# Shared-expert gate and up products of a transformer block: float32 operands replaced by two scaled float16 parts

## The chip, the cores and the metric

The kernel is one program on one core of a Trainium2 chip. The core has a matrix engine (TensorE, PE in the rows, with its weight loads as PEld), a vector engine (VectorE, DVE), an activation engine (ScalarE, ACT), a general engine (GpSimd, POOL), a sequencer that issues most of the DMAs here (SyncE, SP), and 16 DMA engines. Each engine runs its own list of instructions in order; semaphores tie the lists together. The metric is device time in microseconds (us), less is better, as the median of several runs.

## What is computed

The block takes x of 2 x 2048 tokens with 256 channels and gives x of the same shape. Cut to what matters:

```
x = x + ga * attention(layernorm(x) * (1 + ca) + sa)       # 16 heads of 16, q/k/v/o with LoRA parts
h = layernorm(x) * (1 + cb) + sb                           # sa ... gb: modulation, per batch
shared = (silu(h @ shared_gate.T) * (h @ shared_up.T)) @ shared_down.T      # 512 hidden
logits = h @ gate_w.T ; e = argmax(logits) ; s = sigmoid(max(logits))       # 8 experts, one per token
routed = swiglu_e(h * s)                                   # expert e's own gate, up and down weights
x = x + gb * (shared + routed)
```

The change concerns `h @ shared_gate.T` and `h @ shared_up.T`: 4096 tokens x 256 channels x 512 outputs, twice.

## The kernel before, in words

The program has five stages, each written as one function per engine (`attend_tensor`, `attend_vector` and so on).

**Setup and projection** (until about 130 us): adapters are folded into the weights, q, k and v are made.

**Attention** (`attend_*`) runs over 32 heads (16 heads x 2 batches), 37 us a head. For each head TensorE makes the products whose row maxima VectorE finds (`max_product` L1237, `reduce_pair` L1374, 32 pairs m of two blocks a head), up to two heads ahead of the head that is being weighed. Three PSUM banks form a ring between the two: TensorE may not write the next block before VectorE (or, for one block in eight, ScalarE, L1416) has released a bank. Between these blocks TensorE issues, in an order written by hand in `turn`, the scores (L1293) that ScalarE exponentiates (L1437) and the weighing of v by them (L1305). GpSimd has small tasks once a head (`attend_gpsimd`) and a few large ones in named heads: it adds a bias to rows of x (L1490) and divides heads by their sums (L1532). SP loads what later stages need in the function `prepare(n)`.

**Merge** (`merge_*`, from about 1305 us) runs over 8 groups g of 512 tokens: output projection (L1652), residual (DVE L1721), layernorm statistics, normalized rows `n2` (ACT L1764), transposition of them (PE L1661), modulation into `h2T` (ACT L1772, `take`), router logits. Its last part holds the gate and up products of group 0 and the routing on VectorE (`route_vector`). SP stores `x1` and `n2` to DRAM here, loads `wgT`, and then the expert weights: `rgT`, `ruT` and `rdT`, 17 transfers of 512 KB (L1598 to L1602).

**Shared expert** (`shared_*`, 1362 to 1514 us). A group needs four units of gate and up (`gate_up`, L1622: in a unit 2 weights x 2 halves of the 256 channels, 512 columns each), ScalarE's silu (L1981), VectorE's product `hid` (L1825), and `down` (L1959). TensorE's order is gate_up(g+1), down(g), gate_up(g+2), down(g+1) and so on, and it may be at most two units ahead of VectorE: a unit waits until `s_gu_free` shows that the unit two before it has been multiplied. VectorE's order is residual(g) (L1996, then L2000, which needs the loaded rows `xr` of group g), and only then `hid` for group g+2. After the last group's units and down(6) comes the transposition of the first routed tile (L2065, it needs that tile's rows `xs`), then down(7), then the routed experts.

Beside this, GpSimd scatters the 32 tiles of normalized rows into expert order (`scatter_gpsimd`, L1929 to L1942), four buffers `sc_x` deep. SP feeds both: its list (`shared_sync`) is `token_rows` (four loads of `sc_x`, L1894, each of which waits until the scatter from that buffer has landed) in turn with `store(g)` (L1898) and `load(g+2)` (the rows `xr`, L1888). So the order is token_rows(0), load(0), load(1), token_rows(1), then for g in 0 to 2: token_rows(2g+2), store(g), load(g+2), token_rows(2g+3); then store(3), load(5), the wait for all scatters, four loads of `xs` (L2050), store(4), load(6), store(5), load(7), store(6), store(7).

**Routed experts** (`routed_*`, to the end): 39 tiles of 128 rows, each with its expert's weights (L2086, L2109).

## Time and profile before

| | us |
|---|---|
| median of the runs before (1747.12 to 1748.29) | 1747.13 |
| the profiled execution, device time | 1743.12 |
| its span in the trace | 1741.1 |
| TensorE busy | 1681.1 (97%) |
| VectorE busy | 1374.7 (79%) |
| ScalarE busy | 1332.6 (77%) |
| GpSimd busy | 333.1 (19%) |

Times in the trace run from the start of the span. A row of the order of time gives the start, the length, the engine, the line, the operation, its tiles and, in square brackets, how long the engine sat idle before it and what ended the idling. SPq is SP's DMA queue; a row of it is the issue, not the transfer. A matmul's end is modelled, so its pace is read from one start to the next.

### The profile page before, as it was taken

How to read it: one execution, taken by the hardware profiler on the slowest of the kernel's cores; microseconds unless marked ns; L12 is line 12 of the kernel's file. 1: busy time of each engine (PE TensorE's matmuls, PEld its weight loads, DVE VectorE, ACT ScalarE, POOL GpSimd, SP SyncE). 2: the span in 40 equal slices, each digit the busy share in tenths (PEclk: the TensorE clock that was granted, in tenths of full speed). 3: DMA queues.
4: the chain of work that ended last, by engine and by line, in shares of the span. 5: the costliest groups of instructions: out<-in, count | busy, mean ns of one | idle time of the engine just before them, and what ended most of it. 6: DMA issues, size and time to landing. Idle time of an engine off the chain costs nothing.

```text
span 1741.1 us, 31097 instructions
## 1 busy us (share of the span) xinstructions
PE 1681.1 (97%) x11097; PEld 650.6 (37%) x11098; DVE 1374.7 (79%) x2723; ACT 1332.6 (77%) x1662; POOL 333.1 (19%) x427
## 2 busy tenths in 40 slices
PE   9999999999999999999999999999989999999997
PEld 5532222222222222222222222222217555799996
DVE  7689999999999999999999999999906422355553
ACT  5449999999999999999999999999997211244442
POOL 5525020040000000000001000001010377133332
PEclk9999999999999999999999999999999999999998
DMA  7322021131110111101322001131025633322221
GB/s 234 99 66 74 30 80 34 70 93 42 43 58 22 31 52 34 34 22 34 92 61 55 22 31 33 48 88 38 27 78 217 266 107 122 118 74 67 66 69 39
DMA packets 76509, 124.93 MB, mean 72 GB/s; under 512 B 15652, under 2 KB 49141, under 8 KB 76252
## 3 DMA queue, kind: packets, MB, share of 16 engines
q1 hardware_dynamic: 67628, 99.33, 18.3%
q0 software_dynamic: 7792, 22.57, 3.9%
q8 instruction: 77, 1.26, 0.3%
q10 hardware_dynamic: 960, 1.34, 0.3%
q14 instruction: 52, 0.43, 0.1%
HBM read 76.50 MB, written 47.21 MB: 71 GB/s over the span
## 4 chain that ended last, share of the span: by engine, by line
PE 82%; DVE 10%; ACT 5%; issue 3%; DMA 0%; POOLq 0%; POOL 0%; ACTq 0%; DVEq 0%
PE ps L1305 27%; PE ps L1237 18%; DVE mx L1374 8%; PE ps L2086 8%; PE ps L1293 8%; PE ps L1622 6%; PE ps L2109 4%; ACT prob L1437 4%; PE ps L1959 3%; PE ps L780 3%; PE ps L1652 2%; PE ps L799 2%; ACT step_sb L1416 1%; PE ps L2065 0%; PE ps L1266 0%
## 5 line engine op out<-in xcount | busy, mean ns | idle before, releaser
L1437 ACT ACTIVATE prob<-ps 128x1024 f32<-128x1024 f32 x1024 | 1000.8, 1049 | 75.0 <-PE ps L1293 74.8
L1374 DVE TENSOR_REDUCE mx<-ps 128x1 f32<-128x512 f32 x1558 | 1000.7, 685 | 64.0 <-PE ps L1237 43.4
L1237 PE MATMUL ps<-k_high,q_high 48*128 48x512 f16 x1803 | 545.5, 383 | 24.3 <-DVE mx L1374 0.2
L1305 PE MATMUL ps<-prob,vs 128*32 128x512 f32 x4096 | 545.5, 605 | 4.3 <-ACT prob L1437 3.5
L1293 PE MATMUL ps<-q_high,k_high 50*128 50x512 f16 x2048 | 419.0, 382 | 1.6 <-ACT prob L1437 1.6
L1237 PEld LDWEIGHTS ps<-k_high,q_high 48*128 48x128 f16 x1803 | 128.9, 93 | 596.6 <-DVE mx L1374 413.4
L1371 DVE CUSTOM_DVE_ANT_0 step_sb<-ps,step_sb 128x512 f32<-128x512 f32 x245 | 166.8, 681 | 0.0
L1293 PEld LDWEIGHTS ps<-q_high,k_high 50*128 50x128 f16 x2048 | 100.4, 94 | 168.5 <-ACT prob L1437 161.3
L1466 POOL CAST mb<-turned_sb 16x128 f16<-16x128 f32 x32 | 9.0, 280 | 768.6 <-ACT turned_sb L1423 755.1
L1416 ACT ACTIVATE step_sb<-ps 128x512 f32<-128x512 f32 x245 | 150.6, 615 | 0.2 <-PE ps L1237 0.2
L1305 PEld LDWEIGHTS ps<-prob,vs 128*32 128x32 f32 x4096 | 80.6, 107 | 167.5 <-issue 140.1
L1981 ACT ACTIVATE sgate<-ps 128x512 f32<-128x512 f32 x32 | 19.1, 597 | 117.4 <-PE ps L1622 117.4
L2135 ACT ACTIVATE esig<-ps 128x512 f32<-128x512 f32 x39 | 23.3, 597 | 111.4 <-PE ps L2086 111.4
L2169 DVE TENSOR_TENSOR ehT<-esig,ps 128x512 f32<-128x512 f32 x39 | 26.8, 688 | 98.9 <-PE ps L2086 98.9
L1237 PE MATMUL ps<-k_step,q_high 48*128 48x512 f16 x245 | 94.7, 386 | 0.0
L1825 DVE TENSOR_TENSOR hid<-sgate,ps 128x512 f32<-128x512 f32 x32 | 22.0, 688 | 72.5 <-ACT sgate L1981 72.1
L2086 PEld LDWEIGHTS ps<-xsT,gate_w 128*128 128x128 f32 x624 | 75.6, 192 | 1.9
L2086 PE MATMUL ps<-xsT,up_w 128*128 128x128 f32 x624 | 76.0, 275 | 0.0
L2086 PE MATMUL ps<-xsT,gate_w 128*128 128x128 f32 x624 | 76.0, 275 | 0.0
L2109 PE MATMUL ps<-rdT,ehT 128*128 x312 | 73.6, 379 | 0.0
L2086 PEld LDWEIGHTS ps<-xsT,up_w 128*128 128x128 f32 x624 | 72.8, 192 | 0.0
L2229 POOL DMA_INDIRECT x_in<-x_rows,cix x39 | 37.7, 967 | 153.0 <-DVE eout L2196 110.0
(195 smaller groups left out, 1407.7 us busy)
## 6 DMA issues: line engine op xcount, KB each, us to landing
qk_parts<-parts SPq DMA_DIRECT2D x32, 256.0 KB, 2.4
k_high<-qk_parts SPq DMA_DIRECT2D x63, 128.0 KB, 2.7
head_out<-head_out_sb SPq DMA_DIRECT2D x31, 256.0 KB, 2.5
sorted_in<-zero_row POOLq DMA_DIRECT2D x13, 390.0 KB, 3.7
xs<-sorted_in SPq DMA_DIRECT2D x39, 130.0 KB
xg<-in_x SPq DMA_DIRECT2D x8, 512.0 KB, 5.4
x_rows<-xg SPq DMA_DIRECT2D x8, 512.0 KB, 5.0
n_rows<-n SPq DMA_DIRECT2D x8, 512.0 KB, 4.0
```

Source lines behind the costliest of these rows:

```text
L780: mm = pe.matmul(ps[:, 2 + n % 2, :], wqkv[:, o // 2, k, (o % 2) * P:(o % 2 + 1) * P], hT[g % CPB][:, k, :], start=(k == 0), stop=(k == 1))
L1237: pe.matmul(ps[:, ring.bank((n, m, u)), :], q_high[p][mine, t * P:(t + 1) * P], keys, start=True, stop=True).then_inc(s_max, 1)
L1293: mm = pe.matmul(ps[:, bank + u, :], k_high[p][mine, kt * P:(kt + 1) * P], q_high[p][mine, i * CH:(i + 1) * CH], start=True, stop=True)
L1305: mm = pe.matmul(ps[32 * j:32 * j + 32, 7, :], vs[buf(h)][:, kt, :], prob[:, (kt + 1) % 2, j * CH:(j + 1) * CH], start=(kt == 0), stop=(kt ...
L1371: dve.tensor_tensor_reduce(step_sb[:], bank, step_sb[:], 1.0, LOWEST, ALU.add, ALU.max, largest).then_inc(s_ring, 1)
L1374: dve.tensor_reduce(largest, bank, AX.X, ALU.max).then_inc(s_ring, 1)
L1416: act.activation(step_sb[:], bank, ACT.Relu).then_inc(s_turned, 1)
L1437: act.activation(prob[:, (kt + 1) % 2, :].rearrange("p (u c n) -> p u c n", u=2, c=2)[:, :, half, :], ps[:, bank:bank + 2, :], ACT.Exp, sc ...
L1622: mm = pe.matmul(ps[:, at, :], w[:, k, fc * P:(fc + 1) * P], h2T[:, k, bass.ds(g * CH, CH)], start=(k == 0), stop=(k == 1))
L1959: mm = pe.matmul(ps[:, DOWN_BANK[u] + t // 2, t % 2 * D:(t % 2 + 1) * D], hid[u][:, fc, t * P:(t + 1) * P], wdT[:, fc, :], start=(fc == 0) ...
L2086: mm = pe.matmul(ps[:, bank, fc * P:(fc + 1) * P], w[u][:, c, fc * P:(fc + 1) * P], xsT[u][:, c, :], start=(c == 0), stop=(c == 1))
L2109: mm = pe.matmul(ps[:, 6 + u, 0:D], ehT[u][:, c, :], rdT[:, bass.ds(e, 1), c, :].squeeze(1), start=(c == 0), stop=(c == FC - 1))
```

## The change

1. The float32 weights `wgT` and `wuT` are no longer held. They are loaded as `raw_gate` and `raw_up` in head 9 of attention, together with `wdT` (three transfers of 512 KB in place of two), and the load of `wgT` in the merge goes.
2. VectorE finds the largest magnitudes of both weights and of the modulation factors in head 12 (`largest_value`, three reductions). SP stores them in head 13 and loads them back, spread to all partitions, in head 14. In head 17 VectorE makes powers of two from them (`ffn_units`, nine small operations in a row).
3. GpSimd scales `colffn` and splits `raw_gate` in head 18 and `raw_up` in head 19, three passes over 128 x 1024 each (`split_weights`), into `wg_parts` and `wu_parts`, a high and a low float16 part.
4. In the merge `h2T` is two buffers of one group each in place of one tile for all. GpSimd splits each group into `h2_parts` (`split_rows`, two operations over 128 x 1024 a group); ScalarE's `take` waits until the group two before has been split.
5. A gate or up product of a half is three float16 matmuls (high x high, high x low, low x high) in place of one float32 matmul. The scales are taken back in ScalarE's silu (`scale=`), in `take_logits`, and in VectorE's `hid` (a scalar_tensor_tensor in place of a tensor_tensor).
6. The last two of the eight `rdT` loads lie where the `h2T` buffers were. They move from the end of the merge's list on SP to behind token_rows(1) of `shared_sync`, behind waits for the last logits and the last split.

```diff
...
-                    for dst, name in ((wuT, "wuT"), (wdT, "wdT")):
+                    for dst, name in ((raw_gate, "wgT"), (raw_up, "wuT"), (wdT, "wdT")):
...
+                if n == TOPS_AT + 1:
+                    sp.wait_ge(s_range, 10)
+                    sp.dma_start(tops_dram, tops[:]).then_inc(s_shared, 16)
...
+        TOP_TURNS = (8, 14, 20)
...
+            dve.tensor_reduce(tops[:, i:i + 1], source, AX.X, ALU.max, apply_absolute_value=True).then_inc(s_range, 1)
...
+                    if n == TOPS_AT and m in TOP_TURNS:
+                        largest_value(dve, TOP_TURNS.index(m))
+                    if n == TOPS_AT + 5 and m == TOP_TURNS[0]:
+                        ffn_units(dve, step)
...
+            step(pool.tensor_tensor(flat, flat, ffn_scale[:, i:i + 1].to_broadcast([P, HALF * F]), ALU.mult))
+            step(pool.tensor_copy(high, flat))
+            pool.tensor_tensor(low, flat, high, ALU.subtract).then_inc(s_range, 1)
...
-            sp.dma_start(wgT[:], io["wgT"]).then_inc(s_shared, 16)
...
-            for e in range(E):
+            for e in range(E - 2):
                 sp.dma_start(rdT[:, e:e + 1], io["rdT"][:, e:e + 1]).then_inc(s_expert_late, 16)
...
-            for w, at in ((wgT, bank), (wuT, bank + 1)):
+            for w, at in ((wg_parts, bank), (wu_parts, bank + 1)):
...
-                    mm = pe.matmul(ps[:, at, :], w[:, k, fc * P:(fc + 1) * P],
-                                   h2T[:, k, bass.ds(g * CH, CH)], start=(k == 0), stop=(k == 1))
+                    for wp, hp in ((0, 0), (0, 1), (1, 0)):
+                        mm = pe.matmul(ps[:, at, :], w[:, wp, k, fc * P:(fc + 1) * P],
+                                       h2_parts[:, bass.ds(g, 1), hp, k, :].squeeze(1), start=(k == 0 and hp + wp == 0),
+                                       stop=(k == 1 and wp == 1))
...
                 act.wait_ge(s_n2T, g + 1)
+                wait(act, s_h2_parts, g - 1)
+                wait(act, s_lgp, g - 1)
...
             token_rows(1)
+            sp.wait_ge(s_lgp, NCH)
+            sp.wait_ge(s_h2_parts, NCH)
+            for e in range(E - 2, E):
+                sp.dma_start(rdT[:, e:e + 1], io["rdT"][:, e:e + 1]).then_inc(s_expert_late, 16)
             for g in range(3):
...
+        def split_rows(pool, step):
...
+                pool.wait_ge(s_h2T, g + 1)
+                step(pool.tensor_copy(high, flat))
+                pool.tensor_tensor(low, flat, high, ALU.subtract).then_inc(s_h2_parts, 1)
...
```

How the instructions stand, at three places. On VectorE in attention, in head 12 around pairs 8 and 14 (`mx` holds the maxima; the ISA rows at L1371, L1393 in the change, are the one block in eight that is folded with `step_sb`), before:

```order
L1371 ISA step_sb,mx_78<-ps,step_sb 128x512
L1371 ISA mx_78 128x1
L1374 TENSOR_REDUCE mx_78<-ps 128x1 x6
L1371 ISA step_sb,mx_78<-ps,step_sb 128x512
L1371 ISA mx_78 128x1
```

and in the change:

```order
L1396 TENSOR_REDUCE mx_79<-ps 128x1 x5
L1416 TENSOR_REDUCE tops<-raw_gate 128x1
L1396 TENSOR_REDUCE mx_79<-ps 128x1
L1393 ISA step_sb,mx_79<-ps,step_sb 128x512
L1393 ISA mx_79 128x1
L1396 TENSOR_REDUCE mx_79<-ps 128x1 x6
L1393 ISA step_sb,mx_79<-ps,step_sb 128x512
L1393 ISA mx_79 128x1
L1396 TENSOR_REDUCE mx_79<-ps 128x1
L1416 TENSOR_REDUCE tops<-raw_up 128x1
```

Each run of reductions is cut once by a reduction over a weight; in head 17 the nine operations of `ffn_units` stand in such a gap all in a row.

On SP at the start of the shared expert (the two rows in front of `sc_x` are the end of the expert weights), before:

```order
L1600 DMA ruT<-in_ruT 128x1024 x8
L1602 DMA rdT<-in_rdT 128x1024 x8
L1894 DMA sc_x_204<-n_rows 128x256
L1894 DMA sc_x_205<-n_rows 128x256
L1894 DMA sc_x_206<-n_rows 128x256
L1894 DMA sc_x_207<-n_rows 128x256
L1888 DMA xr_200<-x_rows 128x1024
L1888 DMA xr_201<-x_rows 128x1024
```

and in the change, up to where token_rows(2) begins:

```order
L1669 DMA ruT<-in_ruT 128x1024 x8
L1671 DMA rdT<-in_rdT 128x1024 x6
...
L1962 DMA xr_210<-x_rows 128x1024
L1962 DMA xr_211<-x_rows 128x1024
L1968 DMA sc_x_214<-n_rows 128x256
L1968 DMA sc_x_215<-n_rows 128x256
L1968 DMA sc_x_216<-n_rows 128x256
L1968 DMA sc_x_217<-n_rows 128x256
L1982 DMA rdT<-in_rdT 128x1024 x2
```

Two of the eight large loads have moved from in front of the first `sc_x` loads to behind the second four; nothing else on SP's list of this stage has moved, the loads of `xr` least of all.

On TensorE, three units in the middle of a group's loop body, before (each matmul is float32):

```order
L1622 MATMUL ps<-h2T,wgT 128x512 x2
L1622 MATMUL ps<-h2T,wuT 128x512 x2
L1617 REGISTER_ALU
L1622 MATMUL ps<-h2T,wgT 128x512 x2
L1622 MATMUL ps<-h2T,wuT 128x512 x2
L1959 MATMUL ps<-wdT,hid_173 128x256 x16
```

and in the change (float16):

```order
L1692 MATMUL ps<-h_parts,wg_parts 128x512 x6
L1692 MATMUL ps<-h_parts,wu_parts 128x512 x6
L1686 REGISTER_ALU
L1692 MATMUL ps<-h_parts,wg_parts 128x512 x6
L1692 MATMUL ps<-h_parts,wu_parts 128x512 x6
L2046 MATMUL ps<-wdT,hid_183 128x256 x16
```

A unit has 12 float16 matmuls where it had 4 float32 ones; `down` is as it was.

## Rows read from the trace of the kernel before

**Rows 1.** Page, part 4: the chain that ended last, shares of the span by line.

```profile
PE ps L1305 27%; PE ps L1237 18%; DVE mx L1374 8%; PE ps L2086 8%; PE ps L1293 8%; PE ps L1622 6%; PE ps L2109 4%; ACT prob L1437 4%; PE ps L1959 3%; PE ps L780 3%; PE ps L1652 2%; PE ps L799 2%; ACT step_sb L1416 1%; PE ps L2065 0%; PE ps L1266 0%
```

**Rows 2.** Windows of one head each: stretch, length, busy PE, PEld, DVE, ACT, POOL, clock, DMA.

```profile
685.80:722.80 37.00, 35.81 (x261) 7.86 (x257) 35.18 (x66) 34.59 (x44) 1.85 (x5) 1.00 0.12 37
796.70:833.90 37.20, 35.82 (x261) 8.02 (x257) 35.49 (x69) 34.59 (x43) 1.85 (x5) 1.00 0.16 50
```

**Rows 3.** Order of time, VectorE, in the second of these heads.

```profile
822.26 0.34 DVE L1071 RECIPROCAL sums<-sums 128x32 f32<-128x32 f32 x1
822.52 0.63 DVE L1374 TENSOR_REDUCE mx<-ps 128x1 f32<-128x512 f32 x1
```

**Rows 4.** Chain of waits in order of time, shared expert: start, us, what.

```profile
1362.45 13.73 PE ps L1622 x32
...
1383.09 13.73 PE ps L1622 x32
...
1507.15 6.91 PE ps L1959 x32
...
1514.28 5.81 PE ps L2086 x52
```

**Rows 5.** Groups by shape, VectorE, 1300 to 1500 us: busy us, mean ns, idle before.

```profile
L1857 DVE TENSOR_REDUCE segs<-cmp 128x8 f32<-128x256 f32 x1 | 0.4, 420 | 0.0
...
L1858 DVE COPY segs<-segs 128x8 f32<-128x8 f32 x1 | 0.2, 172 | 0.0
```

**Rows 6.** Groups by shape, GpSimd, whole span.

```profile
L1012 POOL TENSOR_TENSOR parts<-qf,parts 128x512 f16<-128x512 f32 x24 | 27.8, 1159 | 45.8 <-ACT parts L877 37.4 <-DVE v_all L545 8.3
...
L962 POOL CAST step_parts<-k_from 128x512 f16<-128x512 f32 x4 | 2.4, 610 | 0.3
```

**Rows 7.** Order of time, ScalarE, merge.

```profile
1336.05 1.43 ACT L1772 ACTIVATE h2T<-ps,colffn 128x512 f32<-128x512 f32 x2
...
1341.11 1.45 ACT L1772 ACTIVATE h2T<-ps,colffn 128x512 f32<-128x512 f32 x2
```

**Rows 8.** Order of time, SP's queue (issues).

```profile
1349.30 4.15 SPq L1600 DMA_DIRECT2D ruT<-in_ruT  x8
...
1359.10 4.95 SPq L1894 DMA_DIRECT2D sc_x<-n_rows  x4
...
1437.54 0.32 SPq L1888 DMA_DIRECT2D xr<-x_rows  x1
...
1465.26 0.32 SPq L1888 DMA_DIRECT2D xr<-x_rows  x1
...
1487.35 1.77 SPq L2050 DMA_DIRECT2D xs<-sorted_in  x4
```

**Rows 9.** Tile xr, issue at 1465.3 us.

```profile
DMA to landing us min/median/max: 3.2/3.5/3.9
```

**Rows 10.** Order of time, GpSimd, scatter.

```profile
1374.72 1.41 POOL L1929 TENSOR_TENSOR sc_x<-sc_x,rowmod 128x256 f32<-128x256 f32 x2 [84.97 <-DMA sc_x<-n_rows]
...
1456.27 1.02 POOL L1942 DMA_INDIRECT sorted_in<-sc_x,slot  x1 [0.16 <-POOL sc_x L1936]
...
1462.80 1.02 POOL L1942 DMA_INDIRECT sorted_in<-sc_x,slot  x1 [0.16 <-POOL sc_x L1936]
...
1471.93 1.03 POOL L1942 DMA_INDIRECT sorted_in<-sc_x,slot  x1 [0.16 <-POOL sc_x L1936]
...
1484.69 0.96 POOL L1942 DMA_INDIRECT sorted_in<-sc_x,slot  x1 [0.30 <-issue]
```

**Rows 11.** Order of time, VectorE, around 1469 us.

```profile
1469.15 1.23 DVE L2000 TENSOR_TENSOR xr<-xr,ymod 128x1024 f32<-128x1024 f32 x1 [2.05 <-DMA xr<-x_rows]
1470.57 0.69 DVE L1825 TENSOR_TENSOR hid<-sgate,ps 128x512 f32<-128x512 f32 x1 [0.20 <-DVE xr L2000]
```

**Rows 12.** Windows, after TensorE's last work (ends near 1729): columns as in rows 2.

```profile
1733.00:1734.00 1.00, 0.00 (x0) 0.00 (x0) 0.00 (x0) 0.00 (x0) 0.00 (x0) 0.50 0.00 0
```

**Rows 13.** Groups by shape, TensorE, 0 to 10 us.

```profile
L628 PE MATMUL ps<-zero_row,ones 128*128 128x256 f32 x13 | 5.0, 549 | 1.6 <-DVEq L660 1.6
```

More of the change, by code:

```diff
@@ L60 @@
 MAX_UNIT = 2.0 ** 15
+WEIGHT_UNIT = 2.0 ** 14
+ROW_UNIT = 2.0 ** 10
+TINY = 2.0 ** -100
 PART_UNIT = 2.0 ** 11
@@ L1467, in split_maxima, with split_weights @@
             pool.tensor_tensor(mb[p][:, 1, :], turned_sb[:], mb[p][:, 0, :], ALU.subtract).then_inc(s_mb, 1)
+        def split_weights(pool, step, raw, w_parts, i):
+            flat = raw[:].rearrange("p k f -> p (k f)")
+            high, low = (w_parts[:, part].rearrange("p k f -> p (k f)") for part in range(2))
+            step(pool.tensor_tensor(flat, flat, ffn_scale[:, i:i + 1].to_broadcast([P, HALF * F]), ALU.mult))
+            step(pool.tensor_copy(high, flat))
+            pool.tensor_tensor(low, flat, high, ALU.subtract).then_inc(s_range, 1)
         def attend_gpsimd(pool, step):
@@ L1921, in shared_sync @@
             store(7)
+        def split_rows(pool, step):
+            for g in range(NCH):
+                high, low = (h2_parts[:, g, part].rearrange("p k t -> p (k t)") for part in range(2))
+                flat = h2T[g % 2][:].rearrange("p k t -> p (k t)")
+                pool.wait_ge(s_h2T, g + 1)
+                step(pool.tensor_copy(high, flat))
+                pool.tensor_tensor(low, flat, high, ALU.subtract).then_inc(s_h2_parts, 1)
         def scatter_gpsimd(pool, step):
```

105 lines of the change are left out of this document (78 added, 27 removed).

## Prediction, made before the change was run

> **What bounds the kernel now.** I read the page's chain first: 82 hundredths of the way that ended last lie on TensorE, and the lines that the change touches hold little of it: gate and up (L1622) 6%, `down` (L1959) 3% [rows 1]. So there are two questions: how much of that 6% comes back, and what the work added beside attention costs, where most of the chain lies.
>
> In attention a head takes 37.0 us, with TensorE busy 35.8, VectorE 35.2 and ScalarE 34.6 of it [rows 2]. No engine is the bound alone; they are coupled through a ring of three banks, and each has about two microseconds to spare in a head. The test for what added VectorE work costs stands in the trace: one head carries eight reciprocals of 0.34 us (0.26 from start to start) [rows 3], 2.1 us in all, and takes 37.2 us [rows 2]. So 0.24 of each 0.26 is absorbed.
>
> In the shared expert the chain is TensorE without a gap: 13.73 us of gate and up and 6.91 of `down`, 20.64 a group [rows 4]. But the other lists are not far behind, and this decides the case. VectorE waited 2.05 us for `xr` of group 4 at 1469.15 [rows 11], which costs nothing now, because TensorE may be two units ahead. And the last scatter is issued at 1484.69 [rows 10] and the rows of the first routed tile are loaded at 1487.35 [rows 8], some 20 us before TensorE turns them (just before the 1507.15 of down(7)) [rows 4].
>
> **The change, part by part.**
>
> *Gate and up.* A group's 16 float32 products of 512 columns take 13.73 us [rows 4], 0.858 each. Taken as four passes over the array, that is 0.2145 a pass; three float16 passes make 0.644, a group 10.30 and a unit 2.57. That saves 3.43 a group on TensorE, 27.5 for eight. The trace has no float16 product of 128 rows with a new 128 x 128 weight for each; the bounds are three passes as above, and a unit as long as before (nothing saved). I take the first: the float32 weight loads are hidden in the same lines already.
>
> *Group 0 and the start.* Its units lie in the merge between transpositions and router logits, where TensorE waits for ScalarE; from the order of time I get about 1.4 us of the 3.4, so that gate_up(1) starts near 1360.7 in place of 1362.45 [rows 4]. As will be seen, it is worth nothing.
>
> *What is late next.* SP's list is not changed as to `xr`. The load for group 3 is issued at 1437.54, for group 4 at 1465.26 [rows 8], and lands 3.5 us later [rows 9]; they stand there because they are queued behind `token_rows`, whose loads wait for GpSimd's scatters. With 17.2 us a group in place of 20.64, down(3) ends near 1430 and down(4) near 1448 or, after a first stall, 1456. VectorE then waits in residual(3) until 1441 and in residual(4) until 1469, and `hid` of the groups 5 and 6 is queued behind it on its list. TensorE has run its two units ahead and waits for `s_gu_free`: about 7 us in group 5 and 11 in group 6. So the end of this stage hangs on the landing of `xr` for group 4, not on the matmuls. From there: landing 1468.8, the addition at 1469.15 for 1.23 [rows 11], `hid` 0.2 later for 0.69 [rows 11], which frees TensorE at 1471.3; then two units 5.15, down(5) 6.91, gate_up(7) 10.30, down(6) 6.91, the transposition 0.22, down(7) 6.91 and 0.22: 1507.9, where the routed experts start now at 1514.28 [rows 4]. That is a gain of 6.4. Residual(5) doesn't bind again: its load is issued at 1480.83 or earlier, and TensorE has finished down(5) only at 1483.
>
> *The clock after a stall.* At the end of the trace, in the fifth microsecond after TensorE's last work, the granted clock is 0.50, the 1.2 GHz level [rows 12]. Stalls of 7 and 11 us are longer, so TensorE comes back at 1.2 GHz. What the return costs is seen at the start: 13 matmuls of 256 columns in 5.0 us [rows 13], 0.386 each, where `down` takes 6.91 for 32 records, 0.216 [rows 4]: 2.0 us too much until the clock is back. After the first stall this is hidden in the second; after the second it is not: +1.8 (0 to 2.0).
>
> *The two `rdT` loads.* From 1349.3 to the landing of the first `sc_x` (1374.72, when GpSimd begins) 17 loads of 512 KB pass [rows 8, 10], 1.5 us each. Two fewer in front let the scatters begin 3.0 us earlier. Behind token_rows(1) the same two come back: two scatters take 6.5 us from start to start, and 9.1 where a 512 KB store and load stand between (1462.80 to 1471.93) [rows 10]. That is 2.6, elsewhere 1.8; I take 2.1 (0 to 3.0). Everything after, `xr` for group 4 with it, is 0.9 earlier (0 to 3). The shared stage thus gains 6.4 - 1.8 + 0.9 = 5.5, with bounds at 4.4 and 9.4.
>
> *VectorE in attention.* Two reductions over 1024 elements: 1.23 each by the addition of the same width [rows 11], 1.15 from start to start; one small, 0.1; nine operations of `ffn_units` in a row, of which the first over 384 elements 0.5 (0.42 for 256 [rows 5]) and eight at 0.17 [rows 5] with a semaphore between, 0.2 each: 2.1. In all 4.5. Behind each stand the reductions that release the ring; TensorE waits for them, and the scores behind it on its list. If the ring absorbs 0.24 of an insertion, whatever its length, the cost is 0.9 + 0.9 + 0 + 1.85 = 3.65. If the head absorbs 92% of the sum, as it did with eight short ones, it is 0.4; if nothing is absorbed, 4.5. I take 3.65, since a lump of 1.15 is longer than the 0.6 of one bank, and what TensorE and ScalarE have lost they don't regain at an unchanged cadence.
>
> *GpSimd in attention.* A split of 128 x 1024: a product 2.4, a cast twice 0.61, a subtraction twice 1.16 [rows 6], 6 us, in head 18 and again in 19. They are issued at the start of a head, and what is queued behind them, `split_maxima`, gets its input some 27 us later. Cost 0; without that cover it would be 6 each. The loads on SP (one more of 512 KB, and the two small ones) are hidden the same way.
>
> *GpSimd in the merge.* A group's split is a cast 1.2 and a subtraction 2.3 [rows 6], 3.5 us, where `take` comes every 5.06 us (1336.05 to 1341.11) [rows 7] and the wait is for the group two before. Cost 0. All eight are done near 1358, before SP's `sc_x` has landed. The Trainium skill (GPSIMD Engine Reference, Specifications) says that GpSimd shares its SBUF interfaces with VectorE and contends with VectorE instructions that have two SBUF inputs or run in a two-port mode. The subtraction of rows 6 ran in the projection, beside VectorE's normalizations of rows in SBUF, and took 1.159; I see no contention there. What the rule would do here is the third rival.
>
> *The sum.* -5.5 + 3.65 = -1.85 us: 1741.3 against the profiled execution's 1743.12. The median of the runs shown, 1747.13, is 4.0 above that execution; on it the forecast is **1745.3**. The measurement can tell a change of about 0.2%, 3.5 us, from none.
>
> **The rivals.**
>
> 1. *Attention absorbs the added work* (cost 0.4): -5.1, 1742.0. For it: the head with eight reciprocals. Against: none of those was longer than the slack of one bank.
> 2. *`xr` doesn't bind* (TensorE's wait isn't where I put it). Then the scatters are next: the first tile's rows are loaded at 1487.35 - 0.9 [rows 8], land and are weighed by 1489.5, and down(7) follows; the routed experts start at 1496.9, a gain of 17.4, in all -13.7: 1733.4. For it: the wait of 2.05 costs nothing now. Against: the lists, which say that `hid` stands behind the residual.
> 3. *GpSimd paces the merge: slower than before.* The point is 5.06 us a split [rows 7]; at 3.5 it is hidden. If VectorE's work beside it stretched it to 6, ScalarE's `take` would wait for it from group 2 on, 0.95 a group, and with it the stores that the expert loads and then the scatters follow: +6, in all +4.1, 1751.2. For it: beside these splits VectorE has statistics and products from SBUF. Against: 1.159 beside such work [rows 6]. (The Trainium skill's rule above, GPSIMD Engine Reference, would make this the likely case.)
> 4. *The float16 weight loads are not hidden.* At 0.09 us for each of 12 in a unit, gate and up of a group take 14.6 in place of 13.73; six units (half of group 6 and group 7) behind `xr` make the stage 6.5 longer than forecast: +4.7, 1751.8.
>
> **How the numbers follow.** Forecast 0.52, attention absorbs 0.22, `xr` doesn't bind 0.08, GpSimd paces 0.12, weight loads 0.06. The likeliest one's own range is 1741 to 1748 (its bounds -5.8 and +0.1, with a microsecond or two for the measurement). The range for 8 in 10 takes in rival 1 with its lower bound (-9.0) and rival 3: 1738.0 to 1751.5, and leaves out rival 2 and half of rival 4. Faster by over 0.2%: rivals 1 and 2 and 0.08 of the forecast, 0.38. Slower: 0.19, by rivals 3 and 4 and a remainder. Between: 0.43.
>
> **What would show it.** In the profile after, a gate or up matmul should start every 0.215 us. VectorE should wait for `xr` at the additions of the groups 3 and 4, 9 us or more each, and TensorE sit idle in the gate and up products of groups 5 and 6; the granted clock should fall there and a unit after it be slow. The routed experts should start 5 to 6 us earlier relative to the end of attention, and the first scatters about 3 us. Attention should be 3 to 4 us longer, all of it in the heads 10 to 12 and 15 or 16. ScalarE's `take` should come every 5 us. I am wrong if the idling lies elsewhere, if heads keep to 37.0, or if `take` waits for GpSimd.

## The result and the profile after

The changed kernel takes 1751.17 us in the median (1747.74 to 1755.44, 20 runs), the kernel before 1745.84 beside it on the same chip (1743.52 to 1748.29, 20 runs): a ratio of 1.0030, 95% interval 1.0024 to 1.0037. That is 5.3 us slower where 1.85 less was forecast. The profiled execution of the changed kernel took 1755.44 us with a span of 1753.6. It is the slowest of its 20 runs, and that of before, 1743.12, lies below all 20 of its own. So for the accounting both kernels were profiled once more on one chip (g1 and g2 below), and it goes by that pair.

The chain that ended last, by line, answers to [rows 1]: gate and up (L1692) have gone from 6% to 1%. In their place stand the loads of token rows and the scatters, which it didn't hold before.

```profile
PE ps L1327 27%; PE ps L1259 18%; PE ps L2176 8%; PE ps L1315 8%; DVE mx L1396 8%; PE ps L2199 4%; ACT prob L1491 3%; PE ps L795 3%; DMA sc_x<-n_rows 2%; DMA sorted_in<-sc_x,slot 2%; PE ps L814 2%; PE ps L2046 1%; PE ps L1692 1%; POOL sc_x L2016 1%; ACT step_sb L1470 1%
```

Shared expert of the changed kernel, order of time, VectorE and TensorE (they answer to [rows 4, 11]):

```profile
1444.53 1.46 PE L1692 MATMUL ps<-h_parts,wg_parts 128*128 x6
1445.83 1.46 PE L1692 MATMUL ps<-h_parts,wu_parts 128*128 x6
...
1454.10 1.23 DVE L2090 TENSOR_TENSOR xr<-xr,ymod 128x1024 f32<-128x1024 f32 x1 [10.73 <-DMA xr<-x_rows]
...
1456.33 2.74 PE L1692 MATMUL ps<-h_parts,wg_parts 128*128 x6 [9.05 <-DVE hid L1899]
...
1482.45 1.23 DVE L2090 TENSOR_TENSOR xr<-xr,ymod 128x1024 f32<-128x1024 f32 x1 [10.77 <-DMA xr<-x_rows]
...
1484.69 2.74 PE L1692 MATMUL ps<-h_parts,wg_parts 128*128 x6 [9.27 <-DVE hid L1899]
1487.22 2.77 PE L1692 MATMUL ps<-h_parts,wu_parts 128*128 x6
```

Six float16 matmuls start 1.30 us after the six before them (1444.53 to 1445.83), 0.217 each: the weight loads are hidden. VectorE waits twice, for 10.7 us, for `xr`. `hid` stands behind it on its list, and TensorE sits idle twice, 9.1 and 9.3 us, in the gate and up products of groups 5 and 6. Then a half unit takes 2.53 us from start to start (1484.69 to 1487.22) in place of 1.30. The windows of this kernel say why: stretch, length, busy PE, PEld, DVE, ACT, POOL, granted clock, DMA.

```profile
1450.00:1456.00 6.00, 0.00 (x0) 0.00 (x0) 1.70 (x2) 0.00 (x0) 2.85 (x4) 0.50 0.46 137
1456.00:1458.00 2.00, 1.67 (x4) 0.59 (x5) 0.94 (x2) 0.00 (x0) 1.82 (x4) 0.50 0.14 49
...
1484.00:1490.00 6.00, 5.31 (x13) 1.94 (x14) 1.29 (x2) 0.00 (x0) 4.65 (x8) 0.50 0.26 87
```

The granted clock is 0.50, the 1.2 GHz level, from about 2 us into the first idle stretch and 5 us into the second. Behind the first stall it is back after 3 us, behind the second after not quite 6.

The stages of g1 (before) and g2 (changed), profiled on one chip. The rows are tile groups: count, ns min/median/max, first and last start. First g1:

```profile
L1443 ACT COPY head_out_sb<-ps x32: 585/632/634, 169.5 to 1306.6; 128x512 f32<-128x512 f32 x32
...
L1764 ACT ACTIVATE n<-xg,shift,std x32: 584/588/602, 1313.5 to 1347.0; 128x256 f32<-128x256 f32 x32
...
L2086 PE MATMUL ps<-xsT,gate_w x624: 272/275/275, 1515.8 to 1725.2; 128*128 128x128 f32 x156
```

and g2:

```profile
L1497 ACT COPY head_out_sb<-ps x32: 586/629/629, 168.0 to 1309.9; 128x512 f32<-128x512 f32 x32
...
L1835 ACT ACTIVATE n<-xg,shift,std x32: 584/587/602, 1316.8 to 1353.1; 128x256 f32<-128x256 f32 x32
...
L2176 PE MATMUL ps<-xsT,gate_w x624: 272/275/275, 1519.9 to 1729.3; 128*128 128x128 f32 x156
```

The two stretches between are cut at the first scaled token row (GpSimd, 1376.2 and 1379.6) and at the issue of `xr` for group 4, in g1 and in g2:

```profile
1467.96 0.32 SPq L1888 DMA_DIRECT2D xr<-x_rows  x1
```

```profile
1397.77 0.81 SPq L1982 DMA_DIRECT2D rdT<-in_rdT  x2
...
1475.24 0.32 SPq L1962 DMA_DIRECT2D xr<-x_rows  x1
```

| stretch | g1, before | g2, changed | difference | forecast |
|---|---|---|---|---|
| attention, first to last head copy | 1137.1 | 1141.9 | +4.8 | +3.65 |
| merge, last head copy to last row of n | 40.4 | 43.2 | +2.8 | 0 |
| last row of n to first scaled token row | 29.2 | 26.5 | -2.7 | -3.0 |
| from there to the issue of `xr` of group 4 | 91.8 | 95.6 | +3.8 | +2.1 |
| from there to the first matmul of gate_w | 47.8 | 44.7 | -3.1 | -4.6 |
| gate_w, first to last matmul | 209.4 | 209.4 | 0 | 0 |
| sum | | | +5.6 | -1.85 |

Less 1.5, by which g1 came later into attention (that part isn't touched by the change), the sum is the 4.1 by which the spans differ (1742.8 and 1746.9). The medians of the two differ by 4.9 (1748.58, and 1743.64 of the kernel before beside it).

### The profile page after: what moved, and what is told of

It is laid out like the page before. It is cut to its first block, busy times and chain, and to the rows that moved or that the text cites. A ratio compares the mean times of both kernels' runs of the same rounds, so it can differ in the third digit from the quotient of the medians.

```text
span 1753.6 us, 31410 instructions
## 1 busy us (share of the span) xinstructions
PE 1667.3 (95%) x11225; PEld 640.7 (37%) x11226; DVE 1384.4 (79%) x2735; ACT 1334.5 (76%) x1662; POOL 369.8 (21%) x450
## 4 chain that ended last, share of the span: by engine, by line
PE 74%; DVE 10%; DMA 6%; ACT 4%; issue 3%; POOL 1%; SPq 1%; POOLq 0%; ACTq 0%; DVEq 0%
PE ps L1327 27%; PE ps L1259 18%; PE ps L2176 8%; PE ps L1315 8%; DVE mx L1396 8%; PE ps L2199 4%; ACT prob L1491 3%; PE ps L795 3%; DMA sc_x<-n_rows 2%; DMA sorted_in<-sc_x,slot 2%; PE ps L814 2%; PE ps L2046 1%; PE ps L1692 1%; POOL sc_x L2016 1%; ACT step_sb L1470 1%
## 5 line engine op out<-in xcount | busy, mean ns | idle before, releaser
L1393 DVE CUSTOM_DVE_ANT_0 step_sb<-ps,step_sb 128x512 f32<-128x512 f32 x245 | 166.5, 679 | 0.0
L1692 PE MATMUL ps<-h_parts,wg_parts 128*128 (+1 forms) x192 | 49.6, 397 | 20.7 <-DVE hid L1899 19.5
```

The source lines that it names most:

```text
L1393: dve.tensor_tensor_reduce(step_sb[:], bank, step_sb[:], 1.0, LOWEST, ALU.add, ALU.max, largest).then_inc(s_ring, 1)
L1692: mm = pe.matmul(ps[:, at, :], w[:, wp, k, fc * P:(fc + 1) * P], h2_parts[:, bass.ds(g, 1), hp, k, :].squeeze(1), start=(k == 0 and hp + w ...
```

## The experiments

Each ratio is to the kernel before, run beside it.

### The parts of the change, one at a time (e1 to e4)

**e1**, the nine operations of `ffn_units` one for every second pair:

```diff
-                    if n == TOPS_AT + 5 and m == TOP_TURNS[0]:
-                        ffn_units(dve, step)
+                    if n == TOPS_AT + 5 and 4 <= m <= 20 and m % 2 == 0:
+                        ffn_unit(dve, step, (m - 4) // 2)
```

> The change with one edit: the nine operations of ffn_units stand one each behind the pairs 4, 6 ... 20 of head 17 in place of all nine behind pair 8. The work is the same. Theory (a lump makes TensorE idle, its clock falls, and the rest of the 4.7 us is the slow clock): no granted clock under 1.00 in attention, that head back to 37.0 to 37.3 us, 4.5 us less than the change, about 1 us over the kernel before. Rival (what counts is the added time on VectorE, 2.4 us, wherever it stands): the head still takes 39 or more, at most 2.3 us less than the change.

Measured: 1748.37 us, ratio 1.0012 (1.0004 to 1.0021), 2.8 less than the changed kernel; the 4.5 of the theory was read from that kernel's slowest run. Attention takes 1139.3 us, 4.1 less than in the changed kernel's first profile. The two heads behind which the operations lie take 37.4 and 37.1, where the nine in a row (the lump) made one of 41.8. What the lump does, in the changed kernel, order of time on VectorE and TensorE, and windows:

```profile
724.04 0.67 DVE L1421 TENSOR_REDUCE largest<-all_tops 128x3 f32<-128x384 f32 x1
...
726.30 0.15 DVE L1431 TENSOR_SCALAR ffn_restore<-top_power 128x1 f32<-128x1 f32 x1
...
727.11 0.39 PE L1259 MATMUL ps<-k_high,q_high 48*128 48x512 f16 x1 [1.54 <-DVE mx L1396]
```

```profile
728.00:732.00 4.00, 4.00 (x21) 0.78 (x18) 3.29 (x6) 3.12 (x4) 0.00 (x0) 0.66 0.63 209
732.00:736.00 4.00, 4.00 (x20) 0.76 (x23) 2.65 (x7) 1.86 (x3) 0.00 (x0) 0.50 0.00 0
736.00:740.00 4.00, 3.87 (x31) 0.88 (x32) 3.31 (x7) 3.56 (x5) 0.00 (x0) 0.99 0.00 0
```

TensorE idles 1.54 us, and within three microseconds the granted clock falls to 0.50. It is back nine microseconds after the gap. The head is 4.8 longer than 37.0; e1 has no such gap, and its clock stays at 1.00:

```profile
700.00:740.00 40.00, 39.17 (x280) 8.87 (x272) 38.63 (x80) 36.82 (x46) 1.60 (x4) 1.00 0.13 37
```

Eight of the profiles have the lump, and the clock doesn't fall in all: this head takes 41.8 in the changed kernel's first profile and in h2, 40.3 in g2 and f3, and 38.9 to 39.0 in e2, e3, f2 and h1. So the lump costs 2.0, and in four of eight profiles 1.3 to 2.8 more. The gap is 1.54 in all eight; what decides whether the clock falls isn't shown.

**e2**, the two late `rdT` loads behind the first routed loads, with their waits:

```diff
             token_rows(1)
-            sp.wait_ge(s_lgp, NCH)
-            sp.wait_ge(s_h2_parts, NCH)
-            for e in range(E - 2, E):
-                sp.dma_start(rdT[:, e:e + 1], io["rdT"][:, e:e + 1]).then_inc(s_expert_late, 16)
...
                 routed_load(sp, (0, n))
+            for e in range(E - 2, E):
+                sp.dma_start(rdT[:, e:e + 1], io["rdT"][:, e:e + 1]).then_inc(s_expert_late, 16)
             store(4)
```

> The change with one edit: the two rdT loads that stand behind token_rows(1) stand behind the loads of the first four xs, after all scatters. Theory (they delay the scatters, and with these the rows xr of group 4 on which the stage hangs): the time from GpSimd's first scaling to the issue of xr for group 4 falls from 96.0 us to 90.5 to 92, and the kernel is 3 to 5 us faster than the change. Rival (their place costs nothing; the 96.0 was a single slow execution): within 1 us of the change.

Measured: 1748.3, ratio 1.0012 (1.0003 to 1.0021), 2.9 less than the changed kernel. First to last scatter takes 107.6 us in place of 111.6 (106.1 before): by this pair of profiles the two loads cost 4.0 where they stand. Other profiles with the loads in that place give 110.4 to 111.3 (f2, f3, g2, h1), but e1 gives 108.1. So the cost is 2.8 to 4.0 in five of six and half a microsecond in the sixth. A piece of the changed kernel's chain of waits shows where it arises; the scatter that landed beside them took 5.57 us, the others in that chain 2.5 to 3.5:

```profile
1394.67 2.51 DMA sorted_in<-sc_x,slot
...
1401.00 5.57 DMA sorted_in<-sc_x,slot
```

**e3**, the stores and loads of `xr` ahead of the token rows as far as the list allows:

```diff
-            for g in range(3):
-                token_rows(2 * g + 2)
-                store(g)
-                load(g + 2)
-                token_rows(2 * g + 3)
-            store(3)
+            store(0)
+            load(2)
+            token_rows(2)
+            store(1)
+            load(3)
+            token_rows(3)
+            store(2)
+            load(4)
+            token_rows(4)
+            token_rows(5)
+            store(3)
             load(5)
+            token_rows(6)
+            token_rows(7)
```

> The change with one edit: on SP's list store(0) and load(2) stand in front of token_rows(2), store(1) and load(3) in front of token_rows(3), store(2) and load(4) in front of token_rows(4), store(3) and load(5) in front of token_rows(6). Theory (the stage hangs on xr for group 4, then on the scatters): VectorE's two waits of 10.7 us go, so does the slow clock after them, TensorE is at the transposition of the first routed tile before its rows are there, and the kernel is 8 to 13 us faster than the change. Rival (the scatters that now have stores among them earlier give it back): 0 to 3 us faster.

Measured: 1746.01, ratio 0.9998 (0.9989 to 1.0007), 5.2 less than the changed kernel, between the theory's 8 to 13 and the rival's 0 to 3. From the last head copy to the first transposition of a routed tile it takes 192.9 us (1308.7 to 1501.6), in the changed kernel 204.0 (1312.9 to 1516.9). But the first matmul of gate_w follows 10.1 us later in place of 7.3: VectorE now waits for the last groups' `xr`, which is loaded behind the routed loads. A part of the wait was only moved.

**e4**, all three:

> The three edits together. If each cause stands by itself the gains add: 4.5 + 3 to 5 + 8 to 13, 15 to 22 us less than the change, 10 to 17 us less than the kernel before, about 1732 us. If the scatters become the only bound, the second edit's gain should be whole here, and the third's as much as the scatters leave. Rival (one of the waits hides another): under 10 us less than the change.

Measured: 1745.16, ratio 0.9993 (0.9985 to 1.0002), 6.0 less than the changed kernel, where the three alone make 10.9: the causes don't add, as the rival had it. TensorE now waits 14.2 us, in two waits, for the first routed tile's rows and behind residuals. VectorE waits 14.1 us for `xr` of the last groups, and ScalarE's gate_w 22.5 for `rdT`. So the end of the shared expert had passed from `xr` of group 4 to the scatters, `xr` of the last groups and the late `rdT`. The queue as a whole was late, not one transfer in it.

### The routed stage, and the merge (f1 to f3, h1, h3)

In the changed kernel's first profile gate_w took 211.8 us from first to last matmul (1524.2 to 1736.0), in e1 to e4 211.9 to 213.8, before 209.4, with a granted clock of 1.00 and no longer instruction on VectorE, ScalarE or GpSimd. In the kernel before and in g2 all tiles but the first take 5.52 us each; in the changed kernel's first profile 16 of 37 take 5.56 to 5.80, and in e1 18 take up to 5.85. There TensorE, with its weight load, waits for VectorE's copy of the turned rows, which in before and g2 it never does. In the changed kernel's first profile, from 1530 to 1720:

```profile
PEld ps L2176 <- DVE xsT L2252: 3.8, 11, 0.4
```

What makes that copy late is what f1, f2, g1, g2 and h3 ask.

**f1**, the kernel before with every later tile 32 bytes further:

```diff
         restore = held("restore", [P, 1])
+        held("pad", [P, 8])
```

> The kernel before with one unused tile of 32 bytes a partition behind `restore`, so that every tile of the later stages lies 32 bytes further, as the new `ffn_restore` makes it in the changed kernel. Nothing is computed otherwise. Question: in the changed kernel and in all its variants so far the routed stage (first to last matmul of gate_w) takes 211.8 to 213.8 us, before 209.4, with the same mean duration of every instruction and the same granted clock. Theory of the address: the shift makes that difference; this kernel's routed stage takes about 211.8 and the time is 1748.3 (2.4 more than the 1745.9 of before). Rival theory of the program: the difference comes from TensorE's longer program or from the moment at which the loop is entered; this kernel's stage takes 209.4 and its time is 1745.9.

Measured: 1743.73, ratio 1.0002 (0.9993 to 1.0011); the stage 209.4. On this chip the address makes no difference; on that of e1 to e4 it wasn't tried.

**f2**, the changed kernel with the four values in one tile:

```diff
-        restore = held("restore", [P, 1])
-        ffn_restore = held("ffn_restore", [P, 3])
+        restores = held("restores", [P, 4])
```

> The changed kernel with `restore` and `ffn_restore` as columns of one tile of four values, so that the tiles behind them lie where they lie before. Nothing else differs. Theory of the address: the routed stage goes from 211.8 back to 209.4 and the time from 1751.2 to 1748.8. Rival theory of the program: the stage stays at 211.8 and the time at 1751.2.

Measured: 1747.01, ratio 1.0021 (1.0012 to 1.0030); the stage 209.4. As f3 shows 209.4 with the shift, this says nothing for the address either. Nor is it the program: g2, the changed kernel unchanged, has 209.4. On this chip f2, which differs from the changed kernel in addresses alone, is 3.3 us slower than before, so the loss is not 5 in each comparison.

> The kernel before, unchanged, for one more profile, to see whether the routed stage (209.4 us in two profiles so far, 211.8 to 213.8 in the changed kernel's first five) is ever longer with it. If the chip sets it: 209.4 where the other kernels of this call show 209.4, about 212 where they show that.

**h3** and g1, the kernel before unchanged, show 209.4 on two chips (1743.61 in its one run and 1744.06). On the chip of e1 to e4 the kernel before has a median of 1745.88, on the two chips of the f, g and h runs 1743.3 to 1743.7. That fits a stage that is 2 us longer there whatever the kernel, but no profile of the kernel before is known to come from that chip. So it stays open. It is no part of the 4.9 us between g1 and g2, where both show 209.4.

**f3**, the subtraction of `split_rows` in four pieces:

```diff
-                pool.tensor_tensor(low, flat, high, ALU.subtract).then_inc(s_h2_parts, 1)
+                size = HALF * CH // 4
+                for at in range(0, HALF * CH, size):
+                    low_piece = pool.tensor_tensor(low[:, at:at + size], flat[:, at:at + size],
+                                                   high[:, at:at + size], ALU.subtract)
+                low_piece.then_inc(s_h2_parts, 1)
```

> The changed kernel with the subtraction of `split_rows` in four pieces of 256 columns in place of one of 1024 (2.13 us). Theory that VectorE is held until the running GpSimd instruction ends: a VectorE instruction with two inputs in SBUF then waits for 0.6 us at most in place of up to 2.1; the longest shift of `normalize2` falls from 2.11 to about 0.8 us, the merge (last head copy to last row of n) from 43.2 to about 41.2 us (40.5 before) and the time from 1751.2 to 1749.2. Rival, that the two engines share a fixed rate and the work of GpSimd costs VectorE the same in pieces or whole: the merge stays at 43.2 and the time at 1751.2.

The waits that it is about, in the changed kernel, VectorE and GpSimd in order of time:

```profile
1326.06 2.13 POOL L2008 TENSOR_TENSOR h_parts<-h2T,h_parts 128x1024 f16<-128x1024 f32 x1
...
1352.40 2.13 POOL L2008 TENSOR_TENSOR h_parts<-h2T,h_parts 128x1024 f16<-128x1024 f32 x1
```

```profile
1327.13 1.61 DVE L1786 TENSOR_TENSOR o_in<-o_in,l_in 32x512 f32<-32x512 f32 x1 [0.49 <-DMA l_in<-inverse_sums]
...
1352.43 2.11 DVE L1809 SCALAR_TENSOR_TENSOR shift<-mv,std 128x4 f32<-128x4 f32 x1
```

An instruction over four elements takes 2.11 us, and ends at 1354.54, where the subtraction that began 0.03 before it ends (1354.53). Before, all eight of its kind take 0.16. The additions of `xg` (one input in PSUM, mean 1.209, before 1.212) and the statistics (0.414 in both) are as they were. In g2 the last of the eight takes 2.12 us too, and the chain of waits goes through it. The same step of the chain in g1 and in g2:

```profile
1345.30 0.17 DVE shift L1738
```

```profile
1349.44 2.13 DVE shift L1809
```

So 2.0 of the 2.8 us by which the merge grew lie in this one step.

In f3 the longest of the eight is 0.67:

```profile
L1809 DVE SCALAR_TENSOR_TENSOR shift<-mv,std x8: 161/424/671, 1316.7 to 1349.5; 128x4 f32<-128x4 f32 x8
```

Measured: 1746.83, ratio 1.0014 (1.0005 to 1.0024). The merge takes 41.6 us (1310.1 to 1351.7) in place of 43.2 (40.5 before), although GpSimd's work grew (four pieces of 0.70 for one of 2.14). So it is mostly how long one GpSimd instruction runs that counts. ScalarE's waits for `shift` in the merge (total, times, longest) say the same. In g1, g2 and f3:

```profile
ACT n L1764 <- DVE shift L1738: 2.5, 6, 0.6
```

```profile
ACT n L1835 <- DVE shift L1809: 5.6, 6, 2.1
```

```profile
ACT n L1835 <- DVE shift L1809: 4.2, 6, 1.0
```

By the total time f3 can't be told from f2.

**h1**, a cast in place of the subtraction:

```diff
-                pool.tensor_tensor(low, flat, high, ALU.subtract).then_inc(s_h2_parts, 1)
+                pool.tensor_copy(low, flat).then_inc(s_h2_parts, 1)
```

> The changed kernel with the subtraction of `split_rows` (two inputs in SBUF, 2.13 us) replaced by a second cast of the same 1024 columns (one input in SBUF, 1.08 us). This leaves the low parts of the rows out, so the gate and up products are not the right ones. Theory that only the GpSimd instruction with two SBUF inputs holds VectorE: no o_in addition of VectorE is over 0.75 us, the shifts of normalize2 are back at 0.16, and the merge (last head copy to last row of n) goes from 43.2 to 40.5 us as before. Rival, that any GpSimd work in SBUF costs VectorE: it falls only to 41.5 to 42, as it did with the subtraction in pieces.

Measured: 1746.18, ratio 1.0015 (1.0006 to 1.0024), the merge 41.2 (1308.7 to 1349.9), between the theory's 40.5 and the rival's 41.5. GpSimd and VectorE in h1:

```profile
1336.67 1.41 POOL L2007 CAST h_parts<-h2T 128x1024 f16<-128x1024 f32 x1 [2.42 <-ACT h2T L1845]
...
1347.27 1.04 POOL L2008 CAST h_parts<-h2T 128x1024 f16<-128x1024 f32 x1
```

```profile
1336.49 0.69 DVE L1786 TENSOR_TENSOR o_in<-o_in,l_in 32x512 f32<-32x512 f32 x1
...
1347.45 0.88 DVE L1809 SCALAR_TENSOR_TENSOR shift<-mv,std 128x4 f32<-128x4 f32 x1
```

The shift ends at 1348.33, with the cast (1348.31). So a cast, with one input, holds VectorE as well; the two SBUF inputs are needed on VectorE's side only. It goes the other way too: the cast that begins while VectorE adds `o_in` takes 1.41 in place of 1.04. My theory, that the subtraction alone does it, falls.

### Which engine's list the shared stage hangs on (f4, g1 to g4, h2)

**f4**: the edits of e1, e2, f2 and f3, and the residual rows on ScalarE's queue:

```diff
-            with act.Fori(1, NCH) as g:
+            for g in range(1, NCH):
                 for fc in range(FC):
                     shared_silu(act, g, fc, gate_scale)
+                    if g >= 2 and fc == 0:
+                        store_residual_rows(act, g - 2)
+                    if g >= 2 and fc == FC - 1:
+                        load_residual_rows(act, g)
```

> The changed kernel with all that has been found put together and one thing new: the operations of `ffn_units` one per two pairs, the subtraction of `split_rows` in pieces, `restore` and `ffn_restore` in one tile, the two late loads of rdT behind the first routed loads, and, new, the stores of xr for groups 0 to 5 and its loads for groups 2 to 7 issued from ScalarE's queue beside the silu of groups 2 to 7, so that they no longer stand behind the token rows in SyncE's queue. Theory that SyncE's order is what binds the shared stage: no wait of VectorE for xr is left, the granted clock stays up, the last scatter is issued near 1480, the first transpose of xs is near 1491, the first matmul of gate_w near 1498.5, and the time is 1730 (15 less than before). Rival, that the shared stage is bound by the scatters and the routed loads themselves: the first transpose of xs stays at 1505 and the time at 1742.

Measured: 1737.04, ratio 0.9960 (0.9946 to 0.9973): 7 less than before, half of what the theory gave. The profile is that of its slowest run, 1740.45. No wait for `xr` is left. The waits of f4 (engine, line, what it waited for: us in total, times, longest) show what took its place:

```profile
ACT gate_w L2240 <- DMA rdT<-in_rdT: 25.8, 1, 25.8
...
PE ps L2162 <- DVE xs L2168: 14.1, 1, 14.1
```

The transposition of the first routed tile waits 14.1 us for its rows. The last scatter is issued at 1496.0, 115.6 us after the first, and the late `rdT` holds gate_w 3 us more (10.2 in place of 7.3 after that transposition). With four buffers a scatter, its landing, the next load and GpSimd's work make a round of four tiles; GpSimd waited 43.0 us for loads, 14.8 of them ahead of the first scatter.

> The kernel before, unchanged, profiled on the same chip as the next three. Question: the routed stage took 209.4 us in the first profile of the kernel before and 211.8 to 213.8 in that of the changed kernel and its first four variants, but 209.4 in all four kernels of the second series, which ran on another chip. Theory that the chip and not the change sets it: here both this kernel and the changed one show the same length of that stage, be it 209.4 or about 212. Rival, that the change does it in some executions: this one shows 209.4 and the next one more. The ratio of the time is 1.000 either way.

> The changed kernel, unchanged, for a profile beside that of the kernel before on the same chip. By the parts found so far: attention +3.5 to +6.5 us (tops 1.5, units 2.0, and up to 3 more where the granted clock falls behind the 1.5 us in which TensorE idles), merge +2.7, from the issue of rgT to the first scaled row -2.5, scatters +5, the rest of the shared stage with its weights' three passes 5 to 6 less, routed stage +0 (theory that the chip sets it) or +2.4 (rival). Ratio 1.003 with the first theory as with the second.

**g1** measured 1744.06, ratio 0.9999 (0.9990 to 1.0008). **g2** measured 1748.58, ratio 1.0029 (1.0018 to 1.0040), so the +5 is repeated on another chip. Their stages are in the table above.

**g3**: f4 with seven buffers for the scattered rows, and `rdT` ahead of the first routed loads:

```diff
-NSC = 4
+NSC = 7
...
-        sc_x = buffers("sc_x", [P, XW], F32, r, NSC)
+        sc_x = buffers("sc_x", [P, XW], F32, r, NSC - 3)
+        sc_x += [Region(nc, at, at + 2048)(f"sc_x{NSC - 3 + i}", [P, XW]) for i, at in enumerate((wo_at, gbo_at, sums_at))]
```

> The kernel with residual rows on ScalarE's queue, in which the last scatter (issued at 1496.0) and the two late loads of rdT (for which ScalarE's first gate_w waited) had become the bound. Now seven buffers for the scattered rows in place of four, three of them in places that woT, gbo and sums have left, and rdT behind the last token rows, ahead of the first routed loads. Theory that the scatters go at the pace of four buffers' round trips (3.7 us a tile, while GpSimd's own instructions are 2.9): the last scatter is issued near 1474, the first transpose of xs comes when the shared stage lets TensorE go, near 1487.5, the first matmul of gate_w near 1495, and the time is 1723 (20 less than before). Rival, that the DMA engines or VectorE's hold on GpSimd set the pace: the scatters end at 1490 or later, and the time is 1734 with only rdT's wait gone.

Measured: **1721.72, ratio 0.9874 (0.9859 to 0.9889)**, 22 us less than before, where 1723 was expected. Its scatters, and pieces of its chain of waits in the shared expert:

```profile
L2037 POOL DMA_INDIRECT sorted_in<-sc_x,slot x32: 963/1024/1827, 1378.5 to 1466.3; - x32
```

```profile
1451.15 10.36 PE ps L1704 x48
1461.51 6.91 PE ps L2054 x32
1468.41 10.36 PE ps L1704 x48
1478.77 6.91 PE ps L2054 x32
1485.68 0.22 PE ps L2167 x2
1485.90 6.91 PE ps L2054 x32
```

TensorE runs without a gap, 17.27 us a group. The scatters end 19.4 us before the transposition; they take 87.8 us in place of 108 to 116 in the changed kernel and its variants with four buffers.

**g4**, the kernel before with the same two repairs of the queues:

> The kernel before with the same two repairs of its queues (residual rows on ScalarE's queue, seven buffers for the scattered rows), its weights and rows in float32 as they were. Theory that in the kernel before TensorE itself sets the end of the shared stage, so that the repairs are worth something only with the three passes: its time stays within 2 us of before, 1743 (TensorE still ends that stage near 1500). Rival, that the repairs would have brought the gain alone: 1735 or less.

Measured: 1743.15, ratio 0.9998 (0.9988 to 1.0007). Its last scatter is issued at 1465.6, and its gate_w starts at 1513.9, as before (1514.1). The repairs alone are worth nothing: TensorE's float32 products set that end.

**h2**, the changed kernel with the seven buffers and nothing else:

> The changed kernel with seven buffers for the scattered rows in place of four and nothing else; the residual rows stay in SyncE's queue, the units in one lump, the subtraction whole, the rdT loads where the change puts them. Theory that the pace of the scatters is what holds the residual rows, and they the shared stage: VectorE's two waits of 10 us for xr go, the last scatter is issued near 1472, the first transpose of xs is near 1491, and the time is 1728 (1721.7 of the kernel with all repairs, plus 3 in attention, 2 in the merge and 1 to 2 for rdT). Rival, that the order in SyncE's queue has to be changed too, since token rows now stand behind stores that wait for residuals: waits of some microseconds stay, and the time is 1735 or more.

Measured: 1728.59, ratio 0.9919 (0.9905 to 0.9932); expected 1728. What VectorE waited for in its shared expert:

```profile
DVE ymod L2091 <- PE ps L2051: 42.8, 8, 5.7
DVE hid L1903 <- ACT sgate L2075: 40.4, 25, 4.2
...
DVE hid L1903 <- DVE xr L2095: 0.2, 1, 0.2
```

No wait for `xr`, though it is loaded from the same place in SP's list: the list moves at the pace of the scatters, and with more buffers it moves in time. One size (with the order in which the buffers are used, which follows from it) turns a loss of 3 to 5 us into a gain of 15.

## Why the prediction failed

**Right.** That the shared stage would hang on the landing of `xr` for group 4, with waits of VectorE at residual(3) and residual(4), idling of TensorE (7 and 11 us forecast, 9.1 and 9.3 seen: the sum is right, each size is off by 2), the fall of the granted clock behind it (+1.8 forecast; 1.9 in g2, 2.8 in the first profile; the rows behind the forecast give 5.0 - 13 x 0.216 = 2.2, not the 2.0 that it took) and hence most of 27.5 us lost. From the issue of that load to gate_w the forecast gives 44.4 us; g2 has 44.7. Right too: three passes at 0.2145 (10.30 a group forecast, 10.36 in g3), the reductions over the weights (1.8 forecast, head of 38.6 for 37.0: 1.6), -3.0 in front of the scatters (-2.7), nothing for GpSimd in attention.

**Luck.** The 1751.17 lies just inside the stated 1738.0 to 1751.5. The upper end came from the rival in which GpSimd is stretched and `take` waits for it, and neither happened; and the range hung on 1747.13, the median of three runs, where twenty give 1745.84. The direction was wrong.

**Wrong**, in the order of their size, against g1 and g2:

1. *GpSimd in the merge: cost 0.* Measured +2.8. This is the step that failed most: a contention that was named and then priced at nothing. I judged the contention by the time of GpSimd's instruction in [rows 6], and looked for a GpSimd that is stretched. In the merge GpSimd's subtraction kept its 2.13, and `take` waited for TensorE alone (1.6 us, in g1 as in g2), not for GpSimd; VectorE's short instructions with two SBUF inputs were held until it ended, ahead of the normalized rows, on the path that sets the end. The slower rival had the pair of engines right, the victim and the price (+6) not. The trace of before held the answer. In [rows 11] VectorE's addition runs from 1469.15 to 1470.38, and GpSimd's product beside it, in order of time, takes 1.40 where its median is 0.72:

```profile
1469.56 1.40 POOL L1929 TENSOR_TENSOR sc_x<-sc_x,rowmod 128x256 f32<-128x256 f32 x1 [2.89 <-DMA sc_x<-n_rows]
```

   and VectorE's addition takes 1.72 where GpSimd's product began first:

```profile
1404.95 0.71 POOL L1936 TENSOR_TENSOR sc_x<-sc_x,rowmod 128x256 f32<-128x256 f32 x1
1405.03 1.72 DVE L2000 TENSOR_TENSOR xr<-xr,ymod 128x1024 f32<-128x1024 f32 x1
```

   The Trainium skill (SBUF — State Buffer, Who interferes with whom) says that a VectorE instruction with two SBUF inputs contends with a GpSimd instruction that reads SBUF, and (SBUF: two separate sides) that whichever starts first has the shared ports for the whole instruction while the other fully blocks. The rows above agree in both directions, but for 0.14 us: in each of the five pairs the one that came second ends at the end of the first plus its own length less 0.14. Here that gives 1470.38 + 0.72 - 0.14 = 1470.96 (seen 1470.96) and 1405.66 + 1.23 - 0.14 = 1406.75 (seen 1406.75); for the `shift` of 0.16 it is 1354.55 (seen 1354.54) and in h1 1348.33 (seen 1348.33), for the cast of 1.04 in h1 1338.08 (seen 1338.08). So a short instruction seems to end with the long one. The prediction had cited the contention and set it aside.

2. *The two `rdT` loads: 2.1.* Measured 3.8 in g2; by first to last scatter 4.0 in e2's pair, and only 0.5 by e1. The row behind 2.1 was a store and a load between two scatters; two loads of 512 KB at once held one scatter's landing for 5.57 us. The term was mis-sized, and in most profiles outside its bound of 3.0.

3. *The baseline of `xr`.* From the load to gate_w, 4.6 less was forecast and 3.1 measured, not because of the changed kernel (44.7 for 44.4) but because g1 takes 47.8 where the prediction worked with 49.0 (48.9 to the first matmul). The way from first scatter to that load varies with the execution (86.2 to 88.1 in four profiles of before), and VectorE already waited for it, 2.05 and 3.2 us. From the first scaled row to gate_w the four take 139.4 to 139.8, whenever the load comes, since TensorE sets that end; so items 2 and 3 share one miss of 3.2 us, and how it divides depends on the profile taken for before. A slack read from one execution is good to about a microsecond.

4. *`ffn_units`: 1.85.* The ring's share was right: 2.0 where the clock stays (1.85 forecast). The fall of the clock behind a gap of 1.54 us was missing, 1.3 to 2.8 more in half of the profiles. I had given the clock a term only for the stalls of 7 and 11 us.

Of the other rivals, attention absorbed little (37.0 became 38.6 and 39.0 to 41.8), the float16 weight loads are hidden (1.30 a half unit, all twelve), and `xr` bound. The gain of 13.7 that its rival would have given came only once the scatters' buffers were seven (h2, 14.8 less than before). That the two numbers are close is chance: the rival counted on four buffers and on none of the losses of items 1 and 4. So the prediction's sum was too low by 7.5: 2.8 merge, 1.7 `rdT`, 1.5 baseline, 1.15 attention, 0.3 in front of the scatters.

## What to carry to other kernels

Where work is added on GpSimd, look for VectorE's instructions with two inputs in SBUF beside it, however short: each can be held until the running GpSimd instruction ends, and here the one that was held lay on the path. Cutting GpSimd's instructions into pieces took back 1.5 of 2.8 us. Before an engine is made faster, ask at what pace the lists beside it run: here a buffer count set the pace of a queue that also carried the rows the faster engine would need, and one size changed a loss of 3 to 5 us into a gain of 15. Added work in a coupled ring is best laid one short instruction at a time; a lump that makes TensorE idle may cost its clock as well.

## What was not expected of the hardware

- The granted clock fell to 0.50 behind a gap of 1.54 us in TensorE's work, in four of eight profiles of the same lump (heads of 40.3 to 41.8 for 38.9 to 39.0), and TensorE had been busy before it.
- A VectorE instruction over 4 elements took 2.11 us beside a GpSimd instruction of 2.13, and 0.88 beside a cast of 1.04; each ended within 0.02 us of GpSimd's.
- Beside two loads of 512 KB one scatter landed after 5.57 us, where the others in that chain took 2.5 to 3.5.
- On one chip the kernel before is 2 us slower than on two others (1745.9; 1743.3 to 1743.7), and the four variants of the changed kernel profiled there (e1 to e4) have a routed stage of 211.9 to 213.8 us in place of 209.4. TensorE waits there for VectorE's copy at some tiles; why wasn't found.
